# One layer with 60 experts on one core: the experts' inner units in two tiles of 88 rows, results in two PSUM banks in turn, and a transfer of its own for the second weights

## What is computed

```python
gu = x @ se_gate_up_w.T                                  # shared part, 704 inner units
shared = silu(gu[:, :704]) * gu[:, 704:] @ se_down_w.T * sigmoid(x @ shared_gate_w.T)
probs = softmax(x @ gate_w.T); weights, sel = top_k(probs, 4)
def step(acc, ews):                                      # once for each of the 60 experts
    w13_e, w2_e, cw_e = ews                              # (352, 256), (256, 176), (1024,)
    gu_e = x @ w13_e.T
    h = silu(gu_e[:, :176]) * gu_e[:, 176:]              # 176 inner units
    return acc + cw_e[:, None] * (h @ w2_e.T), None
out = x + gb * (shared + sparse)
```

## Time and profile before

| | |
|---|---|
| median of 3 runs | 431.02 us |
| lowest, highest | 430.18, 434.71 us |
| the profiled execution, first to last instruction (its span) | 458.5 us |
| TensorE busy | 423.1 us (92%), 3449 products |
| VectorE busy | 318.8 us (70%) |
| ScalarE busy | 247.3 us (54%) |
| GpSimd busy | 152.9 us (33%) |
| moved by DMA | 54.81 MB, 20535 packets |
| mean granted TensorE clock | 0.978 of full |

### The profile page before, as it was taken

One profiled execution on the slowest core, in us unless ns is written; L12 is line 12 of the kernel. 1 busy time (PEld: TensorE's weight loads), 2 busy tenths in 40 slices (PEclk: granted clock), 3 DMA queues, 4 the chain that ended last, 5 costly groups with the idle time before them and its releaser, 6 DMA issues.

```text
span 458.5 us, 9187 instructions
## 1 busy us (share of the span) xinstructions
PE 423.1 (92%) x3449; PEld 224.7 (49%) x3449; DVE 318.8 (70%) x739; ACT 247.3 (54%) x406; POOL 152.9 (33%) x177
## 2 busy tenths in 40 slices
PE   8999899999999999999999998987879878979995
PEld 4555323333333333333577776654545545646673
DVE  6878998999999999943476995464544343345457
ACT  1566678788878888887735254333123223233062
POOL 3068201220303030301210008565655764655400
PEclk9999999999999999999999999989979988999998
DMA  8500000000000000000110762488977886896192
GB/s 270 214 4 2 1 1 2 0 2 1 0 1 1 1 1 2 1 1 0 47 36 12 244 245 67 155 283 297 305 258 257 272 299 206 285 286 227 39 375 76
DMA packets 20535, 54.81 MB, mean 120 GB/s; under 512 B 4513, under 2 KB 8825, under 8 KB 20491
## 3 DMA queue, kind: packets, MB, share of 16 engines
q1 hardware_dynamic: 16075, 45.81, 29.5%
q0 software_dynamic: 4416, 8.41, 5.4%
HBM read 49.74 MB, written 8.13 MB: 126 GB/s over the span
## 4 chain that ended last, share of the span: by engine, by line
PE 63%; DVE 12%; another core or an unknown queue 8%; issue 7%; ACT 4%; DMA 4%; POOL 1%; SPq 0%; POOLq 0%; DVEq 0%; ACTq 0%
PE PM L1379 13%; PE EP L1628 7%; PE EP L1366 6%; PE M L1332 6%; PE EP L1369 6%; PE PM L1332 3%; PE EP L1481 3%; PE PM L1650 2%; PE PM L1661 2%; PE EP L1287 2%; DMA w<-ychoice 1%; ACT w L750 1%; PE EP L1303 1%; DMA wide<-in_wmod 1%
## 5 line engine op out<-in xcount | busy, mean ns | idle before, releaser
L670 ACT ACTIVATE QS<-EP 128x1024 f32<-128x1024 f32 x128 | 124.1, 1022 | 24.9 <-PE EP L1369 24.4
L853 DVE TENSOR_REDUCE mx<-M 128x1 f32<-128x512 f32 x171 | 111.6, 684 | 7.2 <-PE M L1332 4.2
L1628 PE MATMUL EP<-w,QS 128*128 128x352 f32 (+1 forms) x244 | 69.9, 497 | 0.0
L1379 PE MATMUL PM<-QS,VA 128*32 128x512 f32 x512 | 68.2, 605 | 0.0
L723 ACT ACTIVATE OT<-EP 128x176 f32<-128x176 f32 x46 | 14.7, 319 | 95.4 <-PE EP L1628 80.6
L853 DVE TENSOR_REDUCE mx<-PM 128x1 f32<-128x512 f32 x85 | 58.1, 684 | 3.8 <-PE M L1332 3.6
L1332 PE MATMUL M<-KT,QT 64*128 64x512 bf16 x171 | 51.4, 384 | 0.2 <-ACT QTB L625 0.2
L1366 PE MATMUL EP<-QT,KT 64*128 64x512 bf16 x256 | 49.0, 377 | 1.0 <-ACT QT L585 0.5
L1369 PE MATMUL EP<-QTB,xh 34*128 34x512 bf16 x256 | 48.9, 377 | 0.0
L525 POOL DMA_INDIRECT QS<-h2rows,tab x26 | 28.6, 1099 | 44.9 <-DVE tab L1073 37.2
L1481 PE MATMUL EP<-segu,QSB 128*128 128x352 f32 x128 | 41.0, 463 | 0.3 <-issue 0.2
(11 more groups left out here) (288 smaller groups left out, 607.3 us busy)
## 6 DMA issues: line engine op xcount, KB each, us to landing
w<-in_w SPq DMA_DIRECT2D x61, 544.0 KB
w<-ychoice SPq DMA_DIRECT2D x8, 512.0 KB, 7.4
segu<-in_segu SPq DMA_DIRECT2D x1, 1408.0 KB, 10.0
x<-in_x SPq DMA_DIRECT2D x2, 512.0 KB, 4.9
wide<-in_wmod SPq DMA_DIRECT2D x1, 1024.0 KB, 7.4
h2rows<-qkv SPq DMA_DIRECT2D x2, 512.0 KB, 2.9
out<-x SPq DMA_DIRECT2D x8, 128.0 KB, 2.3
sedn<-in_sedn SPq DMA_DIRECT2D x1, 640.0 KB, 10.9
```

What stands on the lines that cost most here:

```text
L670: nc.scalar.activation(PT[n % 3][:, 2 * p:2 * p + 2, :], EP[p][:, :, :], ACT.Exp, scale=HD ** -0.5).then_inc(e_done, 1)
L853: nc.vector.tensor_reduce(out=mx[:, u % 2, q, j, c:c + 1], in_=src, axis=AX.X, op=ALU.max).then_inc(m_free, 1)
L1379: ins = mm(PV[HP * j:HP * j + HP, :], VA[:, tt, g, :], PT[n % 3][:, j, :], start=tt == 0, stop=tt == NT - 1)
L1628: ins = mm(BANK[b][lo:lo + n, 0:I13], XGT[b][:, c * P + lo:c * P + lo + n], w[:, r, c * I13:(c + 1) * I13], start=c == 0, stop=c == NC - 1)
```

## The change

- The 176 inner units become two tiles of 88 (`HK`). `hidden_T` on TensorE makes four transposes of 88 units for a pair, for three; `down_own` and `down_rest` are replaced by `down`, which multiplies each of the two tiles with 256 columns of second weights.
- A pair's results take one bank, 256 columns for each block, and pairs take banks 6 and 7 in turn (`Y`). TensorE waits for the results of two pairs before (`e - 4`) for `e - 2`, and for each block's inner copy by itself.
- VectorE copies the inner units with two copies of 88 partitions by 256 columns, each counted in `m_htev`; `m_rest` is gone. The product of the second block is one instruction. In a pair the order becomes: inner copies, product of the first block, results of pair q - 2, product of the second block.
- A load is two transfers: 704 numbers in 128 partitions, and 512 numbers in 88 partitions. The row in memory goes from 1,088 to 1,216 numbers a partition; TensorE waits for a count of 32 a load instead of 16.
- `ovei` and `order` lie in memory that is free at that time (`stats`, `OT`).

```diff
@@ -53,18 +53,11 @@
     NP = NH // 2
     QKV = (NH + 2 * NG) * HD
     NE, TOPK = 60, 4
-    I = (w_in.shape[2] - D - D // 2) // (2 * NC)
+    I = (w_in.shape[2] - 2 * D) // (2 * NC)
     I13 = 2 * I
-    OWN = 112
-    REST = I - OWN
-    OWN_AT = (0, I + REST)
-    HALF = P // 2
-    W_OWN, W_REST = NC * I13, NC * I13 + D
-    WL = W_REST + D // 2
+    HK = I // 2
+    W_2 = NC * I13
+    WL = W_2 + 2 * D
     ISH = segu_in.shape[1] // 2
     SHH = ISH // 2
     NSC = (ISH + P - 1) // P
...
@@ -249,7 +242,7 @@
         PV = BANK[6]
-        YP = [PM[:, :, P * i:P * i + P] for i in range(2)]
+        Y = [BANK[6], BANK[7]]
         MR = [BANK[4], BANK[5], BANK[7]]
...
@@ -356,17 +349,22 @@
                 sp.wait_ge(s_h2, h + 1)
                 sp.dma_start(h2rows[512 * h:512 * h + 512, :].rearrange("(t p) d -> p t d", p=P), AT[:, 4 * h:4 * h + 4, :]).then_inc(h2_st, 16)
+            def weights(x, r, done):
+                sp.dma_start(w[:, r, 0:W_2], w_in[bass.ds(x, 1), :, 0:W_2].rearrange("e p n -> p (e n)")).then_inc(done, 16)
+                sp.dma_start(w[0:HK, r, W_2:WL], w_in[bass.ds(x, 1), 0:HK, W_2:WL].rearrange("e p n -> p (e n)")).then_inc(done, 16)
             def load(k):
                 x = sp.value_load(order[0:1, LOADS[k]:LOADS[k] + 1], min_val=0, max_val=NE - 1)
                 if k >= RING:
                     sp.wait_ge(m_y, BLOCK_OF[k - RING] + 1)
-                sp.dma_start(w[:, k % RING, :], w_in[bass.ds(x, 1), :, :].rearrange("e p n -> p (e n)")).then_inc(ld_w[k % RING], 16)
+                weights(x, k % RING, ld_w[k % RING])
             def overflow_weights(b, done):
                 x = sp.value_load(ovei[0:1, bass.ds(b, 1)], min_val=0, max_val=NE - 1)
-                sp.dma_start(w[:, 0, :], w_in[bass.ds(x, 1), :, :].rearrange("e p n -> p (e n)")).then_inc(done, 16)
+                weights(x, 0, done)
             sp.wait_ge(s_route, 4)
             for k in range(NE):
@@ -1107,49 +1105,40 @@
             def hidden_T(p1, b, experts=2):
                 dve.wait_ge(m_ht, p1)
-                H = BANK[4 + b]
-                nc.vector.tensor_copy(HST[b][0:OWN, 0:experts * P], H[0:OWN, 0:experts * P]).then_inc(m_htev, 1)
                 for i in range(experts):
-                    here, there = slice(REST * i, REST * i + REST), slice(REST * (1 - i), REST * (1 - i) + REST)
-                    nc.vector.tensor_copy(HST[b][there, 3 * P:4 * P], H[here, 2 * P:3 * P])
-                nc.vector.tensor_copy(HST[b][0:experts * REST, 2 * P:3 * P], H[0:experts * REST, 2 * P:3 * P]).then_inc(m_rest, 1)
+                    nc.vector.tensor_copy(HST[b][0:HK, 2 * P * i:2 * P * (i + 1)], BANK[4 + b][0:HK, 2 * P * i:2 * P * (i + 1)]).then_inc(m_htev, 1)
             def hidden(e1, b, pb):
                 dve.wait_ge(m_silu, e1)
-                if b == 0:
-                    nc.vector.tensor_tensor(HS[pb][:, 0:I], SL[b], BANK[b][:, I:2 * I], ALU.mult).then_inc(m_h, 1)
-                else:
-                    nc.vector.tensor_tensor(HS[pb][:, I:I + REST], SL[b][:, OWN:I], BANK[b][:, I + OWN:2 * I], ALU.mult)
-                    nc.vector.tensor_tensor(HS[pb][:, I + REST:2 * I], SL[b][:, 0:OWN], BANK[b][:, I:I + OWN], ALU.mult).then_inc(m_h, 1)
-            def result(e, k, sent, i, until):
+                nc.vector.tensor_tensor(HS[pb][:, I * b:I * b + I], SL[b], BANK[b][:, I:2 * I], ALU.mult).then_inc(m_h, 1)
+            def result(k, sent, y, until):
                 dve.wait_ge(m_y, until)
                 if sent is not None:
                     dve.wait_ge(y_st[k % BUFS], sent)
-                nc.vector.tensor_tensor(YS[k % BUFS].rearrange("p (d n) -> p d n", d=NC), YP[i],
-                                        MOD[:, 1, :].rearrange("p (d n) -> p d n", d=NC), ALU.mult).then_inc(m_yev, 1)
+                nc.vector.tensor_tensor(YS[k % BUFS], y, MOD[:, 1, :], ALU.mult).then_inc(m_yev, 1)
             def results(q):
                 for i in range(2):
                     e = 2 * q + i
-                    result(e, e, 16 * (e // BUFS) if e >= BUFS else None, i, 2 * q + 2)
+                    result(e, 16 * (e // BUFS) if e >= BUFS else None, Y[q % 2][:, D * i:D * i + D], 2 * q + 2)
             shared_out(EARLY - 1)
             for q in range(NBLK // 2):
                 e, b = 2 * q, q % 2
-                if q >= 2:
-                    results(q - 2)
                 if q >= 1:
                     hidden_T(q, 1 - b)
                 hidden(e + 1, 0, b)
+                if q >= 2:
+                    results(q - 2)
                 hidden(e + 2, 1, b)
                 if 2 <= q < NT + 2:
                     weights_of(q - 2)
             last = (NBLK // 2) % 2
+            hidden_T(NBLK // 2, 1 - last)
             results(NBLK // 2 - 2)
-            hidden_T(NBLK // 2, 1 - last)
             results(NBLK // 2 - 1)
             dve.wait_ge(s_over, 1)
             nov_r = dve.value_load(novi[0:1, 0:1], min_val=1, max_val=MAXOV)
...
@@ -1622,7 +1611,7 @@
                 pe.wait_ge(m_xtev, e1)
                 for r, loads, lo, n in lanes:
                     if loads:
-                        pe.wait_ge(ld_w[r], 16 * loads)
+                        pe.wait_ge(ld_w[r], 32 * loads)
                 for c in range(NC):
                     for r, loads, lo, n in lanes:
                         ins = mm(BANK[b][lo:lo + n, 0:I13], XGT[b][:, c * P + lo:c * P + lo + n], w[:, r, c * I13:(c + 1) * I13],
@@ -1631,35 +1620,24 @@
             def hidden_T(e, b, experts=2):
                 pe.wait_ge(m_h, e)
-                H = BANK[4 + b]
-                for i in range(experts):
-                    tr(H[0:OWN, i * P:(i + 1) * P], HS[b][:, OWN_AT[i]:OWN_AT[i] + OWN], I_)
-                tr(H[0:experts * REST, 2 * P:3 * P], HS[b][:, OWN:OWN + experts * REST], I_).then_inc(m_ht, 1)
+                for i in range(2 * experts):
+                    ins = tr(BANK[4 + b][0:HK, i * P:(i + 1) * P], HS[b][:, HK * i:HK * i + HK], I_)
+                ins.then_inc(m_ht, 1)
             def halves_of(lanes):
                 r, loads, lo, n = lanes[0]
                 return lanes if len(lanes) > 1 else [(r, loads, lo, n // 2), (r, loads, lo + n // 2, n // 2)]
-            def down_own(p1, b, blocks):
-                pe.wait_ge(m_htev, p1)
+            def down(first, b, blocks, y):
                 for i, lanes in enumerate(blocks):
-                    for d in range(NC):
+                    pe.wait_ge(m_htev, first + i)
+                    for c in range(2):
                         for r, loads, lo, n in lanes:
-                            mm(BANK[6 + d][lo:lo + n, P * i:P * i + P], HST[b][0:OWN, i * P + lo:i * P + lo + n],
-                               w[0:OWN, r, W_OWN + P * d:W_OWN + P * d + P], start=i == 0, stop=False, skip_group_check=True)
-            def down_rest(p1, b, blocks):
-                pe.wait_ge(m_rest, p1)
-                for i, lanes in enumerate(blocks):
-                    for d in range(NC):
-                        part = slice(HALF * d, HALF * d + HALF)
-                        for r, loads, lo, n in lanes:
-                            o = (2 + (i + d) % 2) * P + lo
-                            ins = mm(BANK[6 + d][lo:lo + n, P * i:P * i + P], HST[b][part, o:o + n], w[part, r, W_REST:WL],
-                                     start=False, stop=True, skip_group_check=True)
+                            o = (2 * i + c) * P + lo
+                            ins = mm(y[lo:lo + n, D * i:D * i + D], HST[b][0:HK, o:o + n],
+                                     w[0:HK, r, W_2 + D * c:W_2 + D * c + D], start=c == 0, stop=c == 1)
                     ins.then_inc(m_y, 1)
             def rows_of(e):
@@ -1694,31 +1672,28 @@
                     transposed(e + 2)
                     transposed(e + 3)
                 gate_up(e + 2, 1, lanes_of(e + 1))
+                if q == 1:
+                    pe.wait_ge(s_sh, EARLY)
+                elif q > 2:
+                    pe.wait_ge(m_yev, e - 4)
                 if q:
-                    if q >= 2:
-                        pe.wait_ge(m_yev, e - 2)
-                    else:
-                        pe.wait_ge(s_sh, EARLY)
-                    down_own(q, 1 - b, blocks_down(q - 1, has_shared(q) or has_shared(q - 1)))
-                    down_rest(q, 1 - b, blocks_down(q - 1, has_shared(q - 1)))
+                    down(e - 1, 1 - b, blocks_down(q - 1, has_shared(q) or has_shared(q - 1)), Y[(q - 1) % 2])
             b = (NBLK // 2) % 2
             hidden_T(NBLK, 1 - b)
             shared_half(EARLY, 1, 1)
-            pe.wait_ge(m_yev, NBLK - 2)
-            down_own(NBLK // 2, 1 - b, blocks_down(NBLK // 2 - 1, False))
-            down_rest(NBLK // 2, 1 - b, blocks_down(NBLK // 2 - 1, False))
+            pe.wait_ge(m_yev, NBLK - 4)
+            down(NBLK - 1, 1 - b, blocks_down(NBLK // 2 - 1, False), Y[1 - b])
             pe.wait_ge(s_over, 1)
```

(22 more changed lines are left out.)

## The result

| | median, us | runs | to the kernel before |
|---|---|---|---|
| before | 431.25 | 430.18 to 434.71 | |
| changed | 459.49 | 457.63 to 461.13 | 1.063 (1.058 to 1.068) |
| changed, again, beside a before of 431.96 | 457.78 | 455.06 to 459.81 | 1.058 (1.053 to 1.064) |

It is slower by about 27 us; the forecast was 8.5. Runs more than 1.5% above the fastest of their kernel are left out of the medians given here, which concerns two of the four runs of one experiment, g2. The runs also met a chip that holds the kernel before at 463.5 us, with TensorE's completions late as in the earlier trace rows; the profile before, 458.5 us long, looks like one of those, while its timed runs and the changed kernel's do not. So rows before and rows after compare two kinds of chip, and only the experiments compare like with like.

A forecast was written before the change was run, and what follows sets the result against it. The prediction took TensorE to bound the kernel, without holes when timed. Its added results columns and transposes, 8.5 us with nothing else counting, took 431.0 to 439.5 us; range 424 to 448.

The forecast's parts named there:

- TensorE's term: TensorE in the expert loop: wider results instructions and a fourth transpose add 0.37 us a pair, 8.5 us over 23 pairs.
- Timed runs have no holes: TensorE in the loop: the profile's 20.5 us of holes are mostly absent when timed; about 4.96 us a pair.
- Rival 1: VectorE's results ahead of the inner copy: holes are real in timed runs, so faster, 425 or 422 us; chance 0.20.
- VectorE's durations: VectorE per pair: inner copies 0.84 us for 1.29, product 0.33, results 0.42 each; 0.6 us less.
- the order: VectorE's inner copies before results: at most 7.6 us off the profiled execution, 0 in a timed run without holes.
- SyncE and DMA: Weight loads: two issues hidden, bytes and packets together -0.05 to +0.1 us a load, neither sign mattering.
- Rival 2: DMA bounds the timed loop, so its slack hides TensorE's 8.5 us: 431 to 434 us; chance 0.17.
- Rival 3: The 88-row transfer spreads unevenly over DMA engines, adding waits for weights of 5 us: 444 to 446 us; chance 0.20.
- The issue distance: SyncE in the loop: loads follow each other by 1.43 us, 4.3 us for a pair with three loads.

The follow-up runs named there:

- g2: The changed kernel with its second transfer over 112 partitions (352 + 224 KB a load): 462.7 us, 1.070 of the kernel before, from two runs.
- f2: The kernel before with each load as two transfers over 128 partitions, of 704 and 384 numbers: 432.28 us, 1.000 of the kernel before.
- f1: The changed kernel with its second transfer over all 128 partitions (352 + 256 KB a load): 438.69 us, 1.015 of the kernel before.
- f4: The changed kernel itself, run again beside a kernel before at 431.96 us: 457.78 us, 1.058.
- e2: The changed kernel with one transfer a load, 1,216 numbers in all 128 partitions (608 KB): 436.73 us, 1.011 of the kernel before.
- e1: The changed kernel with its second transfer over 96 partitions instead of 88: 458.26 us, 1.061 of the kernel before.

## Why the prediction was wrong

- **TensorE's term: right.** +0.37 a pair was forecast and 0.36 to 0.38 measured (5.32 for 4.96 and 5.29 for 4.91); 8.5 us in all, and 9.1 measured with light loads.
- **"Timed runs have no holes": right.** The kernel before without load traffic is 428.3 and has no holes in its trace, so the timed run loses 4 us to loads and holes together, not 20; f2's trace, on a chip with before at 432.0, has no hole for the inner copy either. Rival 1 falls with it.
- **VectorE's durations: right; the order: nothing gained**, as said for a kernel without holes. What I missed is that the order needs the second bank.
- **SyncE and DMA: wrong, and this is the step that failed.** "I bound the two together at -0.05 to +0.1 us a load", "neither sign matters". The price was taken per byte and per packet from loads that all cover 128 partitions. From f1 to f4 it is 19.1 us by 51 loads = 0.37 us a load, with fewer bytes (44.8 MB for 49.8) and fewer packets (22114 for 24859). The term that was left out is how many partitions one transfer covers.
- **Rival 2: half of it is there, once the transfer is a full one.** e2 is 4.5 us slower than before, of the 9.1 that TensorE's work costs. That the rest fills slack which the loads had left is argued from the ledger below, not shown.
- **Rival 3: right in its place, wrong in its mechanism and size.** Late weights are the 18.2 us of holes ahead of gate/up. I had priced it by 11 engines, at half of 9.8 us; with all 16 engines busy (e1, a share of 1.01 to 1.04) it is just as dear, because the busy engines move less (282 to 300 GB/s for 395). And the waits name the weight transfer as releaser, where I had said that no engine would be named.
- **The issue distance** was taken as 1.10 + 0.33 = 1.43 and is 1.87 with 88 rows and 1.61 with 96, 112 or 128. It bounds nothing here: a pair with three loads takes 5.6, the mean pair of 2.7 loads 5.0, under 5.3.

The ledger from 432.0 to 457.8: TensorE +9.1; -4.7 for what the loads had cost the kernel before (4.0) and no longer cost one with a single full transfer (437.4 with light loads, 436.7 with 608 KB, the same within their intervals); +2.0 for the second transfer with its packets (438.7); +19.1 for its 88 partitions. Sum +25.5, for 25.8 measured; the terms come from two chips, with before at 432.3 and 432.0.

No kernel tried that computes the layer beats the one before. 428.3, its time without load traffic, leaves 4 us for anything that does not make TensorE's work less.

## What to carry to other kernels

Here a weight transfer that fills fewer partitions was not cheaper by the rows it leaves out. Price such a one by the rate at which busy DMA engines move it (275 to 300 GB/s here, for 359 to 395), and pad it to 128 partitions or put it in one transfer with its neighbour if the loop's DMA share is near 1. Look at share and GB/s together: a share of 1 at three quarters of the usual rate says that the busy engines get less done, not that there is much to move. And an engine's order may be turned only together with the buffers that its old order kept free.

## What the runs showed that was not expected

- Second weights of 512 numbers a partition: 128 partitions 438.7 us, 88 457.8, 96 458.3, 112 462.7, 64 and 64 483.8 (with a third issue). With the same first transfer, every second transfer of fewer rows and bytes is slower than the full one; 88, 96 and 112 are not told apart beyond their spread (455 to 461, 457 to 461, 460 and 465).
- Splitting a full load into two full transfers costs nothing measurable (432.28 for 431.96), though the packets become as short as 1,536 bytes.
- A load of two transfers is issued every 1.61 us when the second covers 96, 112 or 128 partitions, and every 1.87 when it covers 88.
- One chip holds the same program at 463.5 for 432.0 us, with late completions on TensorE; on it, a change of 1 to 2% in the loop cannot be seen, and one of the order costs more (5.1% for 3.8%).
